# Linear attention with a feed-forward: the scaling of v moved from one GpSimd operation to 24 ScalarE operations

## What is computed

```python
q = causal_dwconv_silu(x @ Wq.T, conv_wq); k = ...; v = ...      # 4 taps
beta = sigmoid(x @ Wb.T); g = -exp(A_log) * softplus(x @ Wa.T + dt_bias)
q = l2norm(q) * DK ** -0.5; k = l2norm(k)
def step(S, inp):
    S = S * exp(gt)
    v_new = vt - einsum('bhk,bhkv->bhv', kt, S)
    S = S + bt * (kt[..., :, None] * v_new[..., None, :])
    return S, einsum('bhk,bhkv->bhv', qt, S)
o = rms(o) * norm_w * silu(x @ Wg.T)
x = layernorm(x + o @ Wo.T)
x = layernorm(x + ternary(x) @ (ternary(W) + rram).T)
```

## Time and profile before

| | |
|---|---|
| median of 3 runs | 430.26 us (430.23 to 431.33) |
| profiled execution | 430.67 us, of which 428.8 us are the span from first to last instruction |
| DVE busy | 322.5 us |
| PE busy | 269.3 us |
| ACT busy | 119.7 us |
| POOL busy | 56.8 us |
| mean granted TensorE clock | 0.759 of full |

### The profile page before, as it was taken

How to read it: one execution, slowest core, us unless ns; L and a number is a source line. 1 busy time by engine, 2 the same in 40 slices (tenths; PEclk the granted TensorE clock), 3 DMA queues, 4 the chain that set the end, 5 groups by cost and what they waited for, 6 DMA issues and landing times.

```text
span 428.8 us, 14040 instructions
## 1 busy us (share of the span) xinstructions
PE 269.3 (63%) x6314; PEld 183.2 (43%) x6314; DVE 322.5 (75%) x790; ACT 119.7 (28%) x245; POOL 56.8 (13%) x63
## 2 busy tenths in 40 slices
PE   3982810698576449795677459785664284986552
PEld 1481600545454217363544336454542263754331
DVE  0765999847698995949798986777989948257996
ACT  0874310056711210356312112357012000232010
POOL 1000360002420200013311100024102000000000
PEclk9965575589777868989676559897686577799686
DMA  7400000000000010000000030000000111000101
GB/s 249 181 0 3 2 0 0 5 2 3 4 3 3 0 50 3 2 3 2 4 3 2 3 98 3 2 3 4 3 2 0 52 50 53 2 5 3 50 0 49
DMA packets 8011, 9.69 MB, mean 23 GB/s; under 512 B 1808, under 2 KB 7056, under 8 KB 7952
## 3 DMA queue, kind: packets, MB, share of 16 engines
q1 hardware_dynamic: 7024, 8.41, 5.9%
q10 hardware_dynamic: 928, 0.39, 0.4%
HBM read 6.70 MB, written 2.10 MB: 21 GB/s over the span
## 4 chain that ended last, share of the span: by engine, by line
DVE 54%; PE 32%; issue 7%; ACT 5%; DMA 1%; DVEq 0%; SPq 0%; ACTq 0%
PE pc L333 7%; PE pj L346 6%; DVE sub_buf L1016 4%; DVE conv_buf L917 4%; PE fr L333 4%; DVE sub_buf L1014 3%; PE pg L457 3%; PE fr L572 2%; PE fr L480 2%; PE pj L457 2%; DVE r_sb L1062 2%; DVE ss L951 2%; DVE stats L1114 2%; DVE r_all L905 1%; DVE t_all L904 1%
## 5 line engine op out<-in xcount | busy, mean ns | idle before, releaser
L917 DVE SCALAR_TENSOR_TENSOR conv_buf<-raw,wconv,conv_buf 128x512 f32<-128x512 f32 x72 | 55.5, 777 | 16.7 <-ACT conv_buf L624 15.1
L346 PE MATMUL pj<-xt,wproj 128*128 128x512 f32 x96 | 54.7, 706 | 8.1 <-DMA xt<-x_t 7.2
L865 POOL TENSOR_TENSOR s_dec<-s_sb,decay 128x192 f32<-128x192 f32 x24 | 14.4, 601 | 216.8 <-DVE s_sb L1071 121.3
L686 ACT ACTIVATE u_sb<-pc 128x192 f32<-128x192 f32 x32 | 10.5, 329 | 114.6 <-PE pc L333 114.6
L333 PE MATMUL pc<-r_sb,t_t 32*32 32x64 f32 x672 | 18.3, 250 | 35.1 <-DVE r_sb L1062 34.3
L333 PE MATMUL fr<-dt_m,chunk_buf 32*32 32x32 f32 x768 | 12.0, 237 | 40.4 <-issue 20.3
L333 PEld LDWEIGHTS pc<-r_sb,t_t 32*32 32x32 f32 x672 | 13.0, 124 | 46.1 <-DVE r_sb L1062 42.8
L346 PEld LDWEIGHTS pj<-xt,wproj 128*128 128x128 f32 x96 | 19.5, 222 | 27.5 <-issue 23.1
L358 PE MATMUL pg<-xt,wproj 128*128 128x512 f32 x48 | 29.3, 739 | 0.0
L333 PEld LDWEIGHTS fr<-dt_m,chunk_buf 32*32 32x32 f32 x768 | 11.2, 151 | 42.0 <-issue 42.0
L457 PE MATMUL pg<-wout,conv_buf 128*128 128x256 f32 x36 | 14.2, 570 | 18.7 <-DVE conv_buf L1108 18.7
(11 more groups left out here) (161 smaller groups left out, 575.8 us busy)
## 6 DMA issues: line engine op xcount, KB each, us to landing
xt<-x_t SPq DMA_DIRECT2D x1, 1536.0 KB, 9.5
x_buf<-x SPq DMA_DIRECT2D x3, 512.0 KB, 3.7
out<-hid_buf SPq DMA_DIRECT2D x6, 256.0 KB, 2.2
wproj<-w_proj SPq DMA_DIRECT2D x1, 1024.0 KB, 8.1
xt<-x_t SPq DMA_DIRECT2D x1, 512.0 KB, 5.9
kq<-x SPq DMA_DIRECT2D x1, 512.0 KB, 3.5
out<-v_tok SPq DMA_DIRECT2D x2, 256.0 KB, 2.1
wout<-w_out SPq DMA_DIRECT2D x1, 384.0 KB, 10.0
```

The lines of the kernel that those rows point to most:

```text
L346: mm = pe.matmul(pj[:, j % 2, :], wproj[:, t, j * P:(j + 1) * P], xt[:, t, k * TOK:(k + 1) * TOK], start=(t == 0), stop=(t == KT - 1))
L686: act.activation(u_sb[:, :, :].rearrange("p g v -> p (g v)"), pc[:, 0:G3 * DV], ACT.Copy).then_inc(u_done, 1)
L865: pool.tensor_tensor(s_dec[:, :, :], s_sb[:, :, :], decay[:, :, c:c + 1].to_broadcast([P, G3, DV]), ALU.mult).then_inc(sdec_done, 1)
L917: e = dve.scalar_tensor_tensor(out=conv[:, d, :, :], in0=raw[:, d, :, m:m + T], scalar=wconv[:, j, m:m + 1], in1=conv[:, d, :, :], op0=ALU ...
```

## The change

rv gets two buffers, used by turns (k % 2). v_scaled leaves POOL. On ACT it becomes 24 operations, one per chunk and group, each over 128 partitions and 64 columns, with the factor as the scale of its partition. In turn k they stand after o_out_of_psum of the chunk: nine at c = 5 (chunks 0 to 2), nine at c = 6 and six at c = 7, the last six ahead of o_square. For pair 0 all 24 stand behind exp_d(0). POOL keeps the small copy of decay under a semaphore of its own, decay_in; it waits for the decay_states of the pair before instead of its last residual and last solve.

```diff
-        rv = sb("rv", [P, G3, NC, DV])
+        rv = sb("rv", [P, 2, G3, NC, DV])
...
-                                 rv[:, g, 0, :] if c == 0 else r_sb[:, g, :], start=True, stop=True)
+                                 rv[:, k % 2, g, 0, :] if c == 0 else r_sb[:, g, :], start=True, stop=True)
...
+            def v_scaled(k, chunks):
+
+                after(act, bv_done, 1, k, 1)
+                after(act, v_tok_done, 1, k, 1)
+                if k > 1:
+                    after(act, r_done, 0, k - 1, NC - 1)
+                    after(act, u_mm, 0, k - 1, NC)
+                for c in chunks:
+                    for g in range(G3):
+                        e = act.activation(rv[:, k % 2, g, c, :],
+                                           v_tok[:, g, c, :, :].rearrange("p h v -> p (h v)"),
+                                           ACT.Identity, scale=bv[:, g * NC + c:g * NC + c + 1])
+                if c == NC - 1:
+                    e.then_inc(rv_done, 1)
...
-                    if front and c == 4:
-                        after(act, v_tok_done, 1, k + 1, 1)
+                    if front and c >= 5:
+                        v_scaled(k + 1, ((0, 1, 2), (3, 4, 5), (6, 7))[c - 5])
...
             exp_d(0)
+            v_scaled(0, range(NC))
...
-            def v_scaled(k):
-                after(pool, bv_done, 1, k, 1)
-                after(pool, v_tok_done, 1, k, 1)
+            def decay_copied(k):
+                after(pool, park_done, 1, k, 1)
                 if not first(k):
-                    after(pool, r_done, 0, k, NC - 1)
-                    after(pool, u_mm, 0, k, NC)
-                pool.tensor_copy(decay[:, :, :].rearrange("p g c -> p (g c)"), park[:, 4, :])
-                pool.tensor_tensor(rv[:, :, :, :].rearrange("p g c v -> p (g c) v"),
-                                   v_tok[:, :, :, :, :].rearrange("p g c h v -> p (g c) (h v)"),
-                                   bv[:, :].unsqueeze(2).to_broadcast([P, U, DV]), ALU.mult).then_inc(rv_done, 1)
+                    after(pool, sdec_done, 0, k, NC - 2)
+                pool.tensor_copy(decay[:, :, :].rearrange("p g c -> p (g c)"), park[:, 4, :]).then_inc(decay_in, 1)
...
-                after(pool, rv_done, 1, k, 1)
+                after(pool, decay_in, 1, k, 1)
...
                 if front:
-                    v_scaled(k + 1)
+                    decay_copied(k + 1)
...
-                    after(dve, rv_done, 0, k, 1)
+                    after(dve, decay_in, 0, k, 1)
...
-                                      rv[:, :, c, :], ALU.add).then_inc(r_done, 1)
+                                      rv[:, k % 2, :, c, :], ALU.add).then_inc(r_done, 1)
```

More of the change, by code:

```diff
@@ L240, in program @@
                              "l21_done", "y32_done"))
-        x32_done, p_mm, p_done, merge_mm, tt_done, rv_done = (
-            sem(n) for n in ("x32_done", "p_mm", "p_done", "merge_mm", "tt_done", "rv_done"))
+        x32_done, p_mm, p_done, merge_mm, tt_done, rv_done, decay_in = (
+            sem(n) for n in ("x32_done", "p_mm", "p_done", "merge_mm", "tt_done", "rv_done", "decay_in"))
         ks_mm, r_done, u_mm, u_done, s_mm, s_done, sdec_done, o_mm, o_out = (
@@ L886, in _ @@
             c_masked(0)
-            v_scaled(0)
+            decay_copied(0)
             for k in range(PAIRS - 1):
```

## The result

The changed kernel takes 424.6 us (median of 4 runs, 424.3 to 424.77), beside 430.25 us of the kernel before (4 runs, 430.2 to 431.33). The ratio is 0.9866, with a 95% interval of 0.9846 to 0.9886: 5.65 us less. The forecast was 422.8 us, 7.5 us less. So the time lies in the stated range of 421.2 to 425.2, but the gain is 1.8 us short, and that is what most of the experiments are about. Medians in this document are of all runs of a kernel, while ratios leave out the runs that took over 1.5% longer than its fastest one, which makes a difference for e8 and e10 alone.

The account below looks back on a forecast made before the run. DVE's queue was taken to bound the kernel, from the substitution to the gated outputs. Three held-up operations, 2.60 + 2.44 + 2.44 = 7.48 us, with all else costing 0, took 430.26 to 422.8 us; range 421.2 to 425.2.

Parts of the forecast that it names:

- The stalls: Three DVE substitution operations held up by POOL's multiplication at the ends of turns 0, 1 and 2: 7.48 us removed.
- The start-up and the copy of decay: Start-up unchanged to the first merge; POOL's 0.20 us copy moves forward in the turn; cost 0 for both.
- the fourth multiplication: POOL's multiplication in the start-up, 57.64 to 60.40; it held no DVE operation, so removing it gains nothing.
- ACT's step: Time from one new ACT operation to the next: 0.18 us taken, 0.30 kept for the range.
- The cover: ACT's idle time at c = 5, 6, 7 and start-up hides the 24 operations; tightest at c = 7, 0.8 or 0.1 us spare.
- The Trainium skill's rule on the shared port: DVE with two SBUF inputs and GpSimd reading SBUF exclude each other; at most one SBUF input is untouched: three stalls.
- rival 4: TensorE's clock: project_out's first products run as fast as later ones, giving 417.1 us; chance 0.04; durations were expected to repeat.
- a tenth or two per turn: Variation of PE's durations, in microseconds per turn either way, giving 422 to 423.6 us around the forecast.
- The forecast's term for PE: PE's project_out follows DVE at an unchanged distance from the merge, so its durations were expected to repeat.

Follow-up runs that it names:

- e8: The kernel before with 6, 4 and 7 unread products of 512 columns ahead of project_out in turns 1, 2 and 3: 422.26 us, ratio 0.9811.
- e10: The kernel of e4 (changed kernel with unread products ahead of project_out) run again, on the chip of e8: 420.54 us, ratio 0.9635 to the kernel before.
- e1: The changed kernel with POOL's multiplication of v put back at its old place, into an unread buffer: 431.3 us, ratio 1.0023 to the kernel before.
- e2: The changed kernel without 23 of the 24 operations on ACT for pairs 1 to 3: 425.04 us.
- e7: The kernel before with two buffers for rv and POOL's whole multiplication moved right behind the last decay_state: 425.49 us, ratio 0.989.
- e12: The changed kernel itself, unaltered, on the chip of e5, e6 and e11: 425.84 us, ratio 0.9875 to the kernel before.
- e4: The changed kernel with 6, 4 and 7 unread products of 512 columns ahead of project_out in turns 1, 2 and 3: 414.54 us, ratio 0.9645.
- e9: The kernel of e4 with two more unread products of 512 columns at c = 4: 420.36 us, ratio 0.9755 to the kernel before.
- e5: The changed kernel with POOL's multiplication put back in turn 1 only: 425.66 us.
- e6: The changed kernel with POOL's multiplication put back in turn 2 only: 425.06 us.
- e11: The changed kernel with two extra unread sums on DVE at the end of turn 0, some 2.45 us together: 425.94 us.
- e3: The changed kernel with POOL's multiplication put back in turn 0 only: 426.37 us.

## Why the prediction was right, and where it was not

- **The stalls.** Forecast 2.60 + 2.44 + 2.44 = 7.48 us; the traces show 2.60 + 2.45 + 2.42 = 7.47. e1 brings them back. They were read correctly as held operations and not as work.
- **The start-up and the copy of decay.** Taking away the fourth multiplication gave nothing: DVE's operation that stood beside it (L1003 now) takes 0.96 us as before. The copy of decay ran at 219.04 for 0.20 us, beside a transpose, and held nobody.
- **ACT's step.** Forecast 0.18, bounds 0.18 to 0.30. Measured, by the row of the start-up:

```profile
51.19 5.83 ACT L723 ACTIVATE rv<-v_tok,bv 128x64 f32<-128x64 f32 x24
```

  With 0.34 us for one operation the step is (5.83 - 0.34) / 23 = 0.24 us. The value that I chose was a quarter too low: 0.18 came from a step of L624 to an operation of another kind, and from a price per column that took off 0.38 us, where L624 and the new operation differ by 0.68 - 0.34 = 0.34 us. The Trainium skill (ScalarE: Activation LUTs, What ACT_TABLE_LOAD costs) gave, as estimates from its figures, 0.24 us for the step and 332 ns for one, and the trace agrees: 338 ns in the mean. The error cost nothing, as 0.59 us were left of the cover.
- **The cover.** Right at all four places; e2 takes the work away and nothing moves.
- **The Trainium skill's rule on the shared port** (SBUF — State Buffer, Who interferes with whom) held in e1 and e7 too, down to which operand lies where.
- **The step that failed** is the last sentence of rival 4: the distance from the merge to project_out doesn't change, so PE's durations repeat. The distance did stay nearly the same. The durations did not: project_out after turn 0 took 5.49 for 4.63 us, after turn 2 5.49 for 4.80, the exponents of turn 1 2.89 for 1.56. The clock's rises and falls did not keep their distance from the work. I gave the clock a chance of 0.04, as a gain, and a tenth or two per turn around the forecast; it was a loss of about 1.8 us, set against 0.4 us won in the start-up. The prediction itself names a project_out that changes its length as a sign of being wrong, and that sign came. In e12 the same code shows another draw: its median, 425.84 us, lies above the upper bound of 425.2, so that 424.6 fell into the range was in part luck. The forecast's term for PE was mis-sized: 0 for an effect that in these traces is up to 1.25 us in project_out and 1.4 us in the exponents of one turn, and that no single execution can give.

What stays open is what lets the clock rise where it does, and with it why the kernels of e8 and e10 scatter over 7 us. That the clock's level goes with the change in PE's durations is shown for all three project_outs, for the exponents and for the feed-forward's products. For the 0.4 us of the start-up there is nothing but that start-ups differ by more than that between executions of one program (2.4 us in e12).

## What to carry to other kernels

An operation of DVE that takes ten times the time of its neighbours of the same shape may be held and not at work: look at what POOL does beside it, and move that to ACT, whose 24 operations held nobody here, or beside operations of DVE that read PSUM (e7). Before trusting a gain on DVE's path, look at which level TensorE's clock has in the stretches that follow; where PE sits idle ahead of a step on the path, products that nobody reads, placed so that they end just before it, were worth more here than the change itself (another 10 us by the median of e4, where the change brought 5.65, though with a wide scatter). Placed where PE's next step comes sooner than they end, they held up the path by 2.6 and 2.15 us in two turns (e9). And a shift of 2 us can be paid back by the clock in the next turn, so judge a small delay by the sum over the whole kernel, in several executions.

## What the runs showed of the hardware

- A delay of 2.5 us on the path that sets the end cost nothing that the times can tell in e5, e6 and e11 and 1.8 us in e3 (426.37 against 424.6, on another chip). In the traces PE's next stretches fell into other parts of the clock's course. The same 12 products of 256 columns took 2.86 us at the upper level, 5.49 at the lower, and all values from 4.2 to 5.2 between when the level changed during them.
- Identical code had its 5.49 us in another turn when its start-up took 2.4 us longer (e12).
- 24 ScalarE operations of 64 columns with a scale per partition followed each other in 0.24 us each, at 0.34 us for one.
